# Attention and mixture-of-experts layer on one Trainium2 core: compact softmax denominators and the last gate chunks in banks of their own

## The reference

```python
def _L0_attn_ref(x, w_qkv, w_out):          # 16 heads of 8 features
    q, k, v = split(x @ w_qkv); to heads
    attn = softmax(q @ k^T / sqrt(128))
    return (attn @ v, heads side by side) @ w_out

def _L0_ffn_ref(x, Wr, Wg, Wu, Wd, Sg, Su, Sd, expert_bias):
    logits = xf @ Wr + expert_bias          # 8 experts, top 2, softmax over the two
    h = silu(xf @ Wg[e]) * (xf @ Wu[e])     # 64 hidden features for each expert
    out = sum over e of rw[:, e] * (h @ Wd[e])
    return out + silu(xf @ Sg) * (xf @ Su) @ Sd

x = x + _layernorm(_L0_attn_ref(_layernorm(x), w_qkv, w_out))
x = x + _layernorm(_L0_ffn_ref(_layernorm(x), Wr, ..., expert_bias))
```

## Time and profile before

| | |
|---|---|
| median of 3 runs | 379.01 us (377.48 to 380.12) |
| the profiled execution's own time | 380.47 us |
| its span, first to last instruction | 378.7 us |
| busy PE / weight loads | 359.4 us / 231.8 us |
| busy DVE / ACT / POOL | 310.7 us / 267.4 us / 200.8 us |
| mean granted clock of PE | 0.993 |

### The profile page before, as it was taken

One profiled execution on the slowest core, in us unless ns is written; L12 is line 12 of the kernel. 1 busy time (PEld: TensorE's weight loads), 2 busy tenths in 40 slices (PEclk: granted clock), 3 DMA queues, 4 the chain that ended last, 5 costly groups with the idle time before them and its releaser, 6 DMA issues.

```text
span 378.7 us, 10110 instructions
## 1 busy us (share of the span) xinstructions
PE 359.4 (95%) x3342; PEld 231.8 (61%) x3342; DVE 310.7 (82%) x788; ACT 267.4 (71%) x511; POOL 200.8 (53%) x518
## 2 busy tenths in 40 slices
PE   7898799999999999999999999999999999999992
PEld 7866556455465557575657565665665566677872
DVE  8476579989899998989998889999998896767461
ACT  4563368788977877887878877786868876964522
POOL 5723121615556374848472835674744655858644
PEclk9999899999999999999999999999999999999998
DMA  2139766847534728557616937544773042222201
GB/s 76 44 105 150 180 123 131 183 140 153 148 105 137 181 54 205 142 144 174 140 58 165 230 103 182 132 121 121 161 181 113 7 115 74 85 74 69 71 8 38
DMA packets 59922, 45.65 MB, mean 121 GB/s; under 512 B 8966, under 2 KB 56966, under 8 KB 59870
## 3 DMA queue, kind: packets, MB, share of 16 engines
q1 hardware_dynamic: 56638, 44.02, 46.5%
q10 hardware_dynamic: 3232, 0.99, 2.3%
HBM read 26.69 MB, written 17.81 MB: 118 GB/s over the span
## 4 chain that ended last, share of the span: by engine, by line
PE 61%; issue 10%; POOL 7%; DMA 6%; DVE 6%; ACT 4%; SPq 3%; ACTq 1%; POOLq 0%; DVEq 0%
PE pvp L674 13%; PE sc L643 8%; PE sc L658 8%; PE bank_d L824 7%; PE bank_d L840 6%; PE bank_d L825 5%; PE bank_d L681 3%; PE bank_a L726 3%; DVE mx L1036 3%; DMA pv_dram<-pv_sb 2%; POOL rstd L1178 2%; POOL hidden L1245 2%; PE bank_d L797 2%; PE bank_a L735 2%; DMA ks<-qk_dram 1%
## 5 line engine op out<-in xcount | busy, mean ns | idle before, releaser
L1036 DVE TENSOR_REDUCE mx<-sc 128x4 f32<-128x1024 f32 x128 | 153.9, 1220 | 20.3 <-PE sc L643 19.4
L888 ACT ACTIVATE pr<-sc 128x1024 f32<-128x1024 f32 x128 | 129.8, 1024 | 32.8 <-PE sc L658 32.3
L674 PE MATMUL pvp<-pr,va 128*32 128x256 f32 x1024 | 68.5, 385 | 0.0
L824 PE MATMUL bank_d<-x3T,wg_sb 128*128 128x256 f32 x160 | 54.8, 424 | 1.3 <-DVE hidden L1134 1.2
L658 PE MATMUL sc<-qs,ks 51*128 51x256 bf16 x512 | 48.8, 274 | 4.1 <-DMA qs<-mT 2.0
L643 PE MATMUL sc<-ks,qs 48*128 48x256 bf16 x512 | 48.9, 274 | 1.1 <-DVE mx L1036 0.7
L1173 POOL TENSOR_TENSOR vareps<-mv,eps 128x2 f32<-128x2 f32 x64 | 12.6, 197 | 67.0 <-DVE mv L1028 67.0
L825 PE MATMUL bank_d<-x3T,wu_sb 128*128 128x256 f32 x160 | 47.6, 379 | 0.0
L1245 POOL TENSOR_TENSOR hidden<-hidden,rwb 128x256 f32<-128x256 f32 x60 | 43.0, 731 | 6.6 <-DMA rwb<-rw_dram 6.3
L1178 POOL TENSOR_TENSOR rstd<-vareps,mhalf 128x2 f32<-128x2 f32 x64 | 44.5, 696 | 0.0
L971 ACT ACTIVATE th<-bank_d 128x256 f32<-128x256 f32 x80 | 30.7, 384 | 18.4 <-PE bank_d L825 16.7
(11 more groups left out here) (113 smaller groups left out, 503.9 us busy)
## 6 DMA issues: line engine op xcount, KB each, us to landing
rwb<-rw_dram SPq DMA_DIRECT2D x30, 256.0 KB, 4.3
qk_dram<-parts SPq DMA_DIRECT2D x30, 192.0 KB, 3.4
qs<-qk_dram SPq DMA_DIRECT2D x30, 192.0 KB, 4.5
ks<-qk_dram SPq DMA_DIRECT2D x30, 192.0 KB, 5.1
qk_dram<-parts SPq DMA_DIRECT2D x30, 128.0 KB, 3.0
pv_dram<-pv_sb SPq DMA_DIRECT2D x14, 256.0 KB, 2.8
x_sb<-in_L_attn_x_dram SPq DMA_DIRECT2D x16, 128.0 KB, 3.0
out_dram<-x SPq DMA_DIRECT2D x16, 128.0 KB, 1.8
```

The source lines that it names most:

```text
L674: mm = pe.matmul(pvp[32 * j:32 * j + 32, g, :], values[:, X * c + 4 * g + j, 32 * tt:32 * tt + 32], pr[:, k, c * N:(c + 1) * N], start=(tt ...
L824: pe.matmul(bank_d[bank][:, 0:N], wg_sb[:, ORDER[n], :], x3T[b % 2][:], start=True, stop=True)
L888: nc.scalar.activation(pr[:, 2 * s:2 * s + 2, :].rearrange("p k n -> p (k n)"), sc[PAIR["s2", b, s]][:].rearrange("p u c n -> p (u c n)"), ...
L1036: nc.vector.tensor_reduce(mx[b % 2][:, :, :, s].rearrange("p c u -> p u c"), sc[PAIR["s1", b, s]][:], AX.X, ALU.max).then_inc(max_done, 1)
```

## The change

For the batches 1 to 14, `den_load` reads only one of each group's eight equal rows, and cuts it in 8 pieces of 32 numbers, so that `den` is [128, 32]. `recip` inverts 128x32 into a new tile `iden`. `rd_spill` writes `iden` to memory, and `rd_load` reads it back with each head's row repeated 8 times into `rden` [128, 256]; `norm` waits for this load instead of for `recip`. Both new DMAs are issued by SP. In the last batch the gate chunks take banks of their own: `sc[1]` in two halves, `bank_d[1]`, `bank_d[0]` and `pvp`; their first products are computed when the attention of all batches is done. The whole table `TIMES` is fitted anew, and with it the fillers: 112 in `FILL` (before 89) and 22 in `FILL_LAST` (before 14). In the new table `load_wgu` stands on ACT behind `part1` of batch 2 and ahead of `v_copy` of batch 2 (before: behind `v_copy` and ahead of `part1` of batch 3), `load_minus` on SP ahead of the first `spill`, and `load_wd` behind `pv_copy` of batch 0 (before: ahead of the first `exp_0`). In the last batch `gu0` stands ahead of `router`. Of the table the diff shows the lines of these steps and of the denominators.

```diff
@@ -33,220 +33,219 @@ TIMES (the table of steps)
...
-    "load_wgu": [1289],
+    "load_wgu": [1099],
-    "load_minus": [1353],
+    "load_minus": [816],
-    "load_wd": [1677],
+    "load_wd": [2440],
-    "recip": [2734, 3744, 4645, 5566, 6313, 7405, 8229, 9363, 10161, 11112, 11968, 12882, 14035, 15069, 15580,
-        16405],
+    "recip": [2542, 3574, 4390, 5171, 6223, 7295, 8116, 8993, 9794, 11022, 11632, 12882, 13917, 14739, 15445,
+        16311],
-    "den_load": [None, 3605, 4469, 5022, 6046, 7215, 7829, 9106, 9911, 10745, 11710, 12693, 13847, 14882, 15441],
+    "den_load": [None, 3400, 4193, 4989, 5959, 7062, 7940, 8827, 9571, 10741, 11462, 12700, 13707, 14462, 15306],
+    "rd_spill": [None, 3592, 4407, 5317, 6240, 7312, 8155, 9011, 9812, 11039, 11650, 12900, 13934, 14757, 15463],
+    "rd_load": [None, 3698, 4514, 5510, 6347, 7487, 8281, 9186, 10034, 11146, 11789, 13006, 14041, 14863, 15569],
-    "norm": [None, 4008, 4735, 5656, 6496, 7610, 8362, 9467, 10328, 11202, 12092, 13112, 14125, 15286, 15882],
+    "norm": [None, 3854, 4657, 5652, 6489, 7629, 8423, 9463, 10360, 11306, 12141, 13150, 14183, 15098, 15711],
-    "wsel": [17449],
+    "wsel": [17282],
...
 
 
 FILL = {
-    "maxT": {0: 10, 1: 1}, "proj": {0: 2}, "qk": {0: 2, 1: 2, 2: 1}, "s1_2": {1: 2, 2: 1}, "s1_3": {1: 3},
-    "s1_4": {0: 2, 1: 3}, "s1_5": {3: 1}, "s1_6": {0: 3, 3: 2}, "s1_7": {0: 3, 1: 1}, "s2_0": {1: 5},
-    "s2_1": {1: 2}, "s2_4": {0: 3, 1: 2}, "s2_5": {0: 2, 1: 2}, "sel1": {0: 3}, "v": {1: 1},
-    "xT": {0: 24, 3: 5, 4: 1},
+    "maxT": {0: 8}, "proj": {0: 3}, "qk": {0: 3, 2: 2, 3: 2}, "s1_0": {1: 2, 2: 1, 3: 1}, "s1_2": {1: 5, 2: 4},
+    "s1_3": {1: 3}, "s1_4": {0: 4}, "s1_5": {0: 4, 2: 2}, "s1_6": {0: 7, 2: 1}, "s2_0": {0: 6}, "s2_1": {0: 2},
+    "s2_2": {0: 2}, "s2_3": {1: 2}, "s2_4": {0: 1}, "s2_5": {1: 4}, "s2_6": {0: 5}, "s2_7": {1: 3}, "sel1": {0: 4},
+    "xT": {0: 24, 2: 2, 3: 3, 5: 2},
 }
 FILL_LAST = {
-    "down": {15: 2}, "gu0": {15: 1}, "gu2": {14: 1, 15: 1}, "gu3": {14: 1, 15: 1}, "gu4": {14: 3},
-    "router": {14: 2, 15: 2},
+    "down": {13: 2, 15: 3}, "gu0": {14: 2, 15: 3}, "gu1": {14: 1}, "gu2": {14: 2, 15: 1}, "gu3": {14: 2, 15: 1},
+    "gu4": {14: 2, 15: 1}, "proj": {15: 2},
 }
...
@@ -339,7 +338,8 @@
         pr = sb("pr", [P, H, TT * N])
         pv_sb = ring(2, "pv_sb", [P, 2, N])
         oc = ring(2, "oc", [P, N])
-        den = ring(2, "den", [P, N])
+        den = ring(2, "den", [P, 32])
+        iden = ring(2, "iden", [P, 32])
         rden = ring(2, "rden", [P, N])
         on = ring(ON_RING, "on", [P, N])
 
@@ -397,6 +397,7 @@
 
         qk_dram = [nc.dram_tensor(f"qk_dram{r}", [2, STACKS, DH, 2, X, N], BF16).ap() for r in range(2)]
         pv_dram = [nc.dram_tensor(f"pv_dram{r}", [2, P, N], F32).ap() for r in range(2)]
+        rd_dram = [nc.dram_tensor(f"rd_dram{r}", [P, 32], F32).ap() for r in range(2)]
         rw_dram = [nc.dram_tensor(f"rw_dram{r}", [4, 32, 32], F32).ap() for r in range(2)]
 
         wqkv_load = sem("wqkv_load")
@@ -412,6 +413,8 @@
         pv_spilled = sems("pv_spilled")
         oc_loaded = sems("oc_loaded")
         den_loaded = sems("den_loaded")
+        rd_spilled = sems("rd_spilled")
+        rd_loaded = sems("rd_loaded")
         rw_spilled = sems("rw_spilled")
         rw_loaded = sems("rw_loaded")
         stored = sems("stored")
@@ -501,6 +504,13 @@
         shift_done = {L: sem(f"shift{L}_done") for L in (1, 2, 3, 4)}
         applied = {L: sem(f"applied{L}") for L in (1, 2, 3, 4)}
 
+        def gu_bank(b, n):
+
+            if b < LAST:
+                return bank_d[BANK[n]]
+            return (sc[1][:, 0].rearrange("p c n -> p (c n)"), sc[1][:, 1].rearrange("p c n -> p (c n)"),
+                    bank_d[1], bank_d[0], pvp[:].rearrange("p g n -> p (g n)"))[n]
+
         block = ctx.enter_context(nc.Block())
 
         def flat(tile):
@@ -586,8 +596,22 @@
                     sp.wait_ge(pv_spilled[b % 2], landed1(1, b))
                     if b >= 2:
                         sp.wait_ge(recip_done, b - 1)
-                    rows = pv_dram[b % 2].rearrange("g (m k) n -> (g m) k n", k=16)
-                    sp.dma_start(den[b % 2][:], rows[:, 8:16, :]).then_inc(den_loaded[b % 2], DMA)
+                    rows = pv_dram[b % 2].rearrange("g (m k) (s t) -> (g m) k s t", k=16, t=32)
+                    sp.dma_start(den[b % 2][:], rows[:, 8]).then_inc(den_loaded[b % 2], DMA)
+                if (b := due(tick, "rd_spill")) is not None:
+                    sp.wait_ge(recip_done, b + 1)
+                    if b >= 3:
+                        sp.wait_ge(rd_loaded[b % 2], landed1(1, b - 2))
+                    sp.dma_start(rd_dram[b % 2], iden[b % 2][:]).then_inc(rd_spilled[b % 2], DMA)
+                if (b := due(tick, "rd_load")) is not None:
+
+                    sp.wait_ge(rd_spilled[b % 2], landed1(1, b))
+                    if b == 2:
+                        sp.wait_ge(direct_norm_done, 1)
+                    if b >= 3:
+                        sp.wait_ge(norm_done, b - 2)
+                    src = rd_dram[b % 2].rearrange("(m k s) t -> m k (s t)", k=1, s=8).broadcast_to([H, DH, N])
+                    sp.dma_start(rden[b % 2][:], src).then_inc(rd_loaded[b % 2], DMA)
                 if (b := due(tick, "pv_load")) is not None and b not in DIRECT:
                     sp.wait_ge(pv_spilled[b % 2], landed1(1, b))
                     if b >= 3:
@@ -819,11 +843,18 @@
                     if (b := due(tick, f"gu{n}")) is not None:
                         fill(f"gu{n}", b)
                         pe.wait_ge(x3T_copied, b + 1)
-                        bank = BANK[n]
-                        turn(d_empty[bank])
-                        pe.matmul(bank_d[bank][:, 0:N], wg_sb[:, ORDER[n], :], x3T[b % 2][:], start=True, stop=True)
-                        pe.matmul(bank_d[bank][:, N:2 * N], wu_sb[:, ORDER[n], :], x3T[b % 2][:], start=True, stop=True).then_inc(gu_done, 1)
-                        d_empty[bank] = (h_done, CHUNKS * b + n + 1)
+                        if b < LAST:
+                            turn(d_empty[BANK[n]])
+                        elif n in (2, 3):
+                            turn(d_empty[3 - n])
+                        else:
+                            pe.wait_ge(pv_copied, NB)
+                            pe.wait_ge(direct_norm_done, 2)
+                        bank = gu_bank(b, n)
+                        pe.matmul(bank[:, 0:N], wg_sb[:, ORDER[n], :], x3T[b % 2][:], start=True, stop=True)
+                        pe.matmul(bank[:, N:2 * N], wu_sb[:, ORDER[n], :], x3T[b % 2][:], start=True, stop=True).then_inc(gu_done, 1)
+                        if b < LAST or n in (2, 3):
+                            d_empty[BANK[n] if b < LAST else 3 - n] = (h_done, CHUNKS * b + n + 1)
                 if (b := due(tick, "down")) is not None:
                     fill("down", b)
                     if b == 0:
@@ -968,7 +999,7 @@
                         act.wait_ge(gu_done, CHUNKS * b + n + 1)
                         if b:
                             act.wait_ge(ha_done, CHUNKS * (b - 1) + n + 1)
-                        nc.scalar.activation(th[n][:], bank_d[BANK[n]][:, 0:N], ACT.Tanh, scale=0.5).then_inc(tanh_done, 1)
+                        nc.scalar.activation(th[n][:], gu_bank(b, n)[:, 0:N], ACT.Tanh, scale=0.5).then_inc(tanh_done, 1)
                 if (b := due(tick, "down_copy")) is not None:
                     act.wait_ge(down_done, b + 1)
                     if b >= 2:
@@ -1059,13 +1090,13 @@
                     nc.vector.tensor_tensor(rest[b % 2][:], bank_a[:].rearrange("p (q n) -> p q n", q=2), parts[b % 2][:, :, 0, :],
                                             ALU.subtract).then_inc(rest1_done, 1)
                 if (b := due(tick, "recip")) is not None:
-                    if b == 2:
-                        dve.wait_ge(direct_norm_done, 1)
-                    if b >= 3:
+                    if b == LAST:
                         dve.wait_ge(norm_done, b - 2)
+                    if b >= 3 and b < LAST:
+                        dve.wait_ge(rd_spilled[b % 2], landed1(1, b - 2))
                     if b not in DIRECT:
                         dve.wait_ge(den_loaded[b % 2], landed1(1, b))
-                        nc.vector.reciprocal(rden[b % 2][:], den[b % 2][:]).then_inc(recip_done, 1)
+                        nc.vector.reciprocal(iden[b % 2][:], den[b % 2][:]).then_inc(recip_done, 1)
                     else:
                         dve.wait_ge(osel_done, 3 if b else 2)
                         nc.vector.reciprocal(rden[b % 2][:], sc[1][:, 0, 0, :] if b else bank_d[0][:, 0:N]).then_inc(recip_done, 1)
@@ -1125,13 +1156,13 @@
                         dve.wait_ge(tanh_done, CHUNKS * b + n + 1)
                         if b:
                             dve.wait_ge(h_done, CHUNKS * (b - 1) + n + 1)
```

(47 more changed lines are left out.)

240 lines of the change are left out of this document (111 added, 129 removed), and 94 rows, old and new, of the table TIMES.

## The result

The changed kernel took 380.32 us (median of 20 runs, 378.49 to 383.58), the kernel before 378.77 (20 runs): ratio 1.0048, 95% interval 1.0024 to 1.0071, so 1.8 us slower (0.9 to 2.7). The forecast was 5.0 us faster, 374.0. The profiled execution took 380.82 us and has a span of 379.0 us. A ratio need not be that of the two medians; where they lie far apart, both are given. The ratios leave out the few slow executions, over 1.5% above the fastest of their kernel (seven in the kernels of the experiments).

What follows compares the result with a forecast made beforehand. PE was taken to bound the middle, DVE close behind. Terms -1.5 + 0.5 - 3.0 + 0 - 1.0 = -5.0 us gave a median of 374.0 us from 379.0; range 369.5 to 380.5.

Steps and rivals of the forecast that it cites:

- rival C: Steady middle: DVE was the bound, so the shorter reciprocal gives -9 us, time 370; chance 0.10.
- (a): Reciprocal on DVE over 32 columns instead of 256: 337 instead of 1743 ns each, worth -1.5 us on PE's path.
- (b): Denominators' second trip through memory: two more DMA issues on SP per batch, divisor 3.0 us later, cost taken as +0.5 us.
- rival D: SP's queue: `rd_spill` and `rd_load` hold back `max_stack` of later batches, so slower, +6 us, time 385; chance 0.08.
- the sign that the prediction gave for D: Middle: PE shows waits for `qs<-mT` or `ks<-qk_dram` of a us and more.
- (c): Order at the start: weights issued earlier, most of PE's stall and slow clock goes, -3.0 us (bounds -6 and +2).
- rival E: Start: weights still in flight when the maxima go out and the clock falls all the same; -1.7 us, 377.3; chance 0.08.
- (d): Order in the middle: PE does the same work in the same mixture, worth 0 (bounds -1 and +2).
- (e): Last gate chunks: own banks, `gu0` to `gu4` in 4.4 instead of 5.15 us, `gu0` ahead of `router`; -1.0 us in all.
- B: No visible change: reciprocal was hidden, start's fillers and late `stack` take back the clock's gain; -1.2 us, 377.8; chance 0.24.

## Why the prediction was wrong, point by point

PE as the bound of the steady part: right. 32 fillers more cost 7.4 us, and 18.3 us less of reciprocals on DVE (13 of 1.41 us) gave 0.4 to 1.7. By a DVE bound the relief would have been worth 9 us, so rival C falls for the old order. The Trainium skill (Perfetto Trace Analysis, Identifying the Most-Contended Engine) judges PE's headroom by MFU or by its weight loads; by these, 60% of the steady part, DVE would be ahead of it: the relief speaks against that in the old order, and the added fillers in the new one.

(a) The reciprocal takes 0.34 us as forecast; DVE is 16.2 us less busy, where about 20 was said. Its relief measured -0.4 by the ratio and -1.7 by the medians, for a forecast of -1.5: not refuted. What I had not seen is that the new order can't do without it.

(b) The step was right in kind: the trip is latency. Landings were 1.8 and 2.6 us. Measured is about +1 in place of +0.5, and not clear of zero. Of its two dangers, SP's queue (rival D) shows one wait of 1.2 us for `qs<-mT` in the steady part. That is the sign that the prediction gave for D, but a single one, and no +11. The other is the projection behind `norm`, which the prediction named and set at nothing: PE waits 0.2 us for it in the changed kernel and 1.67 us in the one without 18 fillers.

(c) This is the step that failed: "Also 23 more fillers stand in the start [...]; they cost nothing only while PE would wait there anyway [...] I take -3.0". It failed on both sides. The price: the same edit that took the hole away filled PE to 17.00 of 17.00 us, so the fillers had no wait to stand in. In the profiled pair 5.0 us of idle time and slow clock went and 5.3 us of fillers came, so the term is about 0 there, and halving the fillers gave back 4.0 us. The gain: stall and slow clock were read from one execution and taken for a property of the order. They went as forecast in the profiled pair (so rival E falls), but two other executions of the same start came through it 1.7 and 2.1 us earlier than the profiled one. Against the average of the three, and with the 1.5 us of work that it leaves for later, the changed start costs some 1.8 us (an estimate from three traces and four) in place of giving 3.0. In the whole the change came out 1.8 us slower where 5.0 faster was said, 6.8 us apart, and 4.8 of them lie in this term. That each filler costs its full length in the start is not shown: without 18, 47 and 88 of them -0.9, 1.4 and 3.0 us were gained. Whether the new order of the start, apart from its fillers, gives anything was not tried.

(d) From the products of batch 2 to those of batch 15 it took 251.8 us in place of 248.3, with a `v` step and three score steps more (the 1.5 us from above). Nine traces with this order and this stretch took 249.7 to 253.8, 251.0 on average; four of the old order 248.0 to 248.8. Less the 1.5 us that is some +1.1 for (a), (b) and (d) together, where -1.0 was forecast. With (a) and (b) as measured that leaves some +0.5 to +2 for (d) alone, where 0 was taken and +2 was the bound. Why one program's middle differs by up to 4 us between traces is open.

(e) `gu0` to `gu4` took 4.63 us (358.85 to 363.48) where 4.4 was forecast; the sum had forgotten that the router now stands between them, 0.36 us. With `gu0` ahead of the router the part gave 1.4 to 2.8 us in place of 1.0. Right, and too small.

Start, middle and end by the traces are +1.8, +1.1 and -1.8 us: +1.1 in all, within the measured +0.9 to +2.7.

The range, 369.5 to 380.5, held the median by 0.2 us; the direction was wrong. Of the rivals B comes nearest: it said that "the additional fillers and the late `stack` take what the clock gives back", but booked -1 for it.

## What to carry to other kernels

Work that is put in only to hold the clock can cost its own length once it has no hole to stand in; halve it and measure, before anything else is tuned. A stall that goes at the same place where filling work comes is one term, not two. A hole that one execution shows may be chance: look at a second trace of the same code before its length is booked as a gain. And an order that was fitted to a short operation can hang on that operation, though the engine's load doesn't say so: measure the part alone in both orders.

## What was not expected of the hardware

The granted clock was 0.50 from 28 to 41 us in the kernel with 24 fillers, where PE was busy for 7.37 us, and 1.00 with 112 fillers, where it was busy for 11.77. Yet the kernel with the 0.50 was faster (0.9970) than the one that held the clock (1.0048). The load of the trip landed within 2.3 to 6.0 us, so a lead that covers its median of 2.6 does not cover it. Runs of one kernel spread by over 5 us (373.7 to 379.3 in the halved one with the weights behind the stack), more than most parts of this change are worth.
